# Narrow heads: stack reads spread over twice as many steps, the maxima's lead raised during the first batch, each stack piece read after its own half is stored

## The reference, cut to what matters

```python
HIDDEN, NUM_HEAD, GROUP = 256, 32, 8
HEAD_DIM = HIDDEN // NUM_HEAD            # 8
REP = NUM_HEAD // GROUP                  # 4
q = hidden_states @ Wq + bq              # (4, 512, 32 heads x 8)
k = hidden_states @ Wk + bk              # (4, 512,  8 heads x 8)
v = hidden_states @ Wv + bv
scores = einsum('bhqd,bhkd->bhqk', q, k) / sqrt(8)
attn = softmax(scores, axis=-1)          # no mask, all 512 x 512
out = einsum('bhqk,bhkd->bhqd', attn, v)
x = x + (out @ Wo + bo)
```

## Time and profile before

| | |
|---|---|
| median of 3 runs | 3807.46 us |
| the profiled execution | 3817.35 us, span 3815.6 us |
| TensorE busy (matmul) | 3340.4 us, 88% |
| VectorE busy | 2627.6 us, 69% |
| ScalarE busy | 1932.8 us, 51% |
| GpSimd busy | 993.4 us, 26% |
| the narrow-head phase: first stack read to last attend | 1257.7 to 1786 us |

### The profile page before, as it was taken

The page is one execution under the profiler, slowest core; times in us unless marked ns, Lnnn a source line. Parts: engine busy times, 40 slices in busy tenths (PEclk is TensorE's granted clock), DMA queues, the critical chain, the costliest instruction groups (busy, mean ns, idle before and its releaser), DMA issues. The chain is left out here.

```text
span 3815.6 us, 62869 instructions
## 1 busy us (share of the span) xinstructions
PE 3340.4 (88%) x21000; PEld 2195.9 (58%) x21002; DVE 2627.6 (69%) x8701; ACT 1932.8 (51%) x5261; POOL 993.4 (26%) x960
## 2 busy tenths in 40 slices
PE   6999999986995898998799999988699558999975
PEld 4666666653553433343567666765355347878864
DVE  6888888874443766774788888877344467777766
ACT  4667676653221355666466767665222115555531
POOL 3212121333443000011221212134344333222213
PEclk9999999997997678999899999998799769999986
DMA  4231300013654222110242310001565500000010
GB/s 125 78 136 55 112 1 1 33 48 122 150 90 100 65 47 56 43 29 17 74 132 82 110 58 1 1 34 59 158 121 88 127 14 15 1 15 4 1 33 23
DMA packets 201926, 234.63 MB, mean 61 GB/s; under 512 B 20358, under 2 KB 188232, under 8 KB 200776
## 3 DMA queue, kind: packets, MB, share of 16 engines
q1 hardware_dynamic: 170664, 190.48, 16.4%
q0 software_dynamic: 30944, 40.14, 6.2%
HBM read 98.13 MB, written 133.73 MB: 61 GB/s over the span
## 5 line engine op out<-in xcount | busy, mean ns | idle before, releaser
L1732 ACT ACTIVATE p_prob<-bank,p_small 128x256 f32<-128x256 f32 (+3 forms) x1280 | 647.4, 516 | 170.7 <-DVE p_small L1903 166.1
L1903 DVE CUSTOM_DVE_ANT_0 bank<-bank,p_mask 128x256 f32<-128x256 f32 (+3 forms) x1280 | 578.5, 489 | 93.5 <-PE bank L1475 82.6
L2248 POOL TENSOR_TENSOR p_tm<-p_rope_a,p_rope_b 128x512 f32<-128x512 f32 x192 | 246.5, 1284 | 1324.2 <-DVE p_rope_b L1883 1319.8
L1475 PE MATMUL bank<-p_k,p_q 64*128 64x256 f32 (+3 forms) x3840 | 528.0, 347 | 18.5 <-ACT p_prob L1732 17.3
L1737 ACT ACTIVATE p_prT<-bank 128x512 f32<-128x512 f32 x752 | 425.1, 601 | 197.7 <-PE bank L1484 196.3
L1484 PE MATMUL bank<-g_ident,p_prob 128*128 128x128 f32 x3008 | 440.2, 286 | 43.7 <-DVE p_prob L1912 18.8
L1912 DVE TENSOR_SCALAR p_prob<-p_prob,p_small 128x256 f32<-128x256 f32 (+3 forms) x1280 | 414.2, 387 | 11.3
L1493 PE MATMUL bank<-p_prT,p_v 128*64 128x512 f32 (+1 forms) x1504 | 420.4, 606 | 0.3 <-ACT p_prT L1737 0.3
L1484 PEld LDWEIGHTS bank<-g_ident,p_prob 128*128 128x128 f32 x3008 | 333.2, 143 | 138.6 <-issue 56.2
L1475 PEld LDWEIGHTS bank<-p_k,p_q 64*128 64x128 f32 (+1 forms) x3840 | 338.3, 188 | 119.8 <-issue 63.0
L1949 DVE TENSOR_REDUCE p_nmax<-bank 128x1 f32<-128x512 f32 x512 | 325.0, 684 | 108.7 <-PE bank L1534 103.4
(11 more groups left out here) (289 smaller groups left out, 6253.6 us busy)
## 6 DMA issues: line engine op xcount, KB each, us to landing
sorted<-p_blank SPq DMA_DIRECT2D x32, 2304.0 KB, 19.2
p_w<-in_L_ffn_w SPq DMA_DIRECT2D x96, 256.0 KB, 4.4
p_h_in<-sorted SPq DMA_DIRECT2D x158, 144.0 KB, 2.7
p_k_st<-k_saved SPq DMA_DIRECT2D x16, 288.0 KB
p_q_st<-q_saved SPq DMA_DIRECT2D x16, 288.0 KB
g_stage<-in_L_ffn_wq SPq DMA_DIRECT2D x8, 512.0 KB, 4.4
g_stage<-in_L_ffn_wo SPq DMA_DIRECT2D x16, 256.0 KB, 5.1
g_res<-first_sum SPq DMA_DIRECT2D x8, 512.0 KB, 7.2
```

Of the source, the lines that this page charges most:

```text
L1475: ins = pe.matmul(h.use.ap[:, 0:n], q[rows, at, :], k[rows, kp, o.g, keys], start=i == 0, stop=i == 2)
L1732: act.activation(s.prob.ap[:, 0:s.o.w], s.use.ap[:, 0:s.o.w], ACT.Exp, bias=sm[:, 0, j:j + 1], scale=-1.0, accum_out=sm[:, 1, j:j + 1]).th ...
L1903: dve.tensor_tensor_reduce(x, x, A.mask[:, A.mask.shape[1] - o.w:], -1.0, FAR, ALU.add, ALU.min, o.sm.ap[:, 0, h.j:h.j + 1]).then_inc(made)
```

## The change

Three edits, all in the narrow-head phase.

1. Between two steps of part 1 of the stack reads, the side stream yields four times, not two, in every batch but the first. So there are eight attend steps from one `r` to the next where there were four.
2. During batch 0, after every eighth attend step one extra step of maxima is recorded. The lead grows from 48 to 64 steps over the batch, and stays there.
3. A step of `small_stack` waits before its read of `q_saved` for the half that holds its own `r`, where it waited for all of it.

```diff
-                    s.b, s.k_saved, s.saved, s.free, s.groups, s.count = b, saved[0], saved, stack_read.get(b - 2), groups, stacked[b % 2][part]
+                    s.b, s.k_saved, s.saved, s.free, s.groups, s.count = b, saved[0], saved[1 + r // 2], stack_read.get(b - 2), groups, stacked[b % 2][part]
                     s.r, s.pace = r, pace[0]
                     if part and b:
-                        yield
-                        yield
+                        for _ in range(4):
+                            yield
...
                     next(peaks, None)
                     if n % 2:
                         next(side, None)
+                    if b == 0 and n % 8 == 7:
+                        next(peaks, None)
...
-            w.wait_ge(*s.saved)
+            w.wait_ge(s.saved)
```

## The result

The changed kernel takes 3842.6 us (median of 4 runs, 3833.65 to 3849.63); the kernel before, run beside it, 3807.09 us. The ratio is 1.0088, with a 95% interval of 1.0068 to 1.0108: **slower by 0.9%**, where a gain of 0.7% was forecast, and outside the range of 3771 to 3796 us. A ratio here isn't the quotient of the two medians, and it leaves out the runs that lie more than 1.5% above the fastest of their kernel, which are two of four in e10 (the profiled one is among them) and two of six in e11. The profiled execution took 3841.22 us.

A forecast was written before the change was run, and what follows sets the result against it. Bound by TensorE, slowed by three waits for the store's DMA and the low clock behind them. Terms -30.0 - 2.4 + 2.6 + 3.0 = -26.8 us from 3807.46 gave 3780.7 us, range 3771 to 3796.

The forecast's parts named there:

- What bounds the kernel: Narrow-head phase: TensorE's three waits for the store's DMA, 13.1 us, and the low clock behind them, 16.9 us.
- Wider spacing: Part 1 stack reads: steps 6.1 us apart for 3.8 us of data, so the queue empties between them; cost nothing.
- Longer lead: Stores of maxima: 14.7 us ahead in batch 0, 23 us later, against landings of 14.0 us; all three waits go.
- What they are worth: The three stretches with store waits: losses of 12.2, 10.1 and 7.7 us, together 30.0 us, all won back.
- The moved maxima: 16 maxima at 0.16 us each on TensorE: 2.6 us added in batch 0, given back in batch 3; sum nothing.
- sign by which the text would have called itself wrong: Attend still waiting for the store in batches 1 or 2, or TensorE waiting for VectorE's queue in batch 0.
- New short waits in batch 0: TensorE: 1.4 us for a `finish` behind a store in bank 7, two `qp` waits of 0.6 us; together 2.6 us.
- Falls of the clock: TensorE in batch 0: a short wait may begin a new clock fall costing 4.0 us; 3.0 us allowed.
- The half's wait: Start of batch 0: `q_saved` reads go out earlier, so the first maximum comes 2.4 us earlier (0 to 2.6).
- The first store is still late: Rival, batch 0: spreading reads doesn't shorten the store's landing, 12.2 us loss stays, 3792.9 us; chance 0.14.
- The waits go, the clock doesn't come back: Rival: other short idle times begin equal clock falls, only 12.9 us of idle won, 3794.6 us; chance 0.13.
- Slower: short waits begin long falls: Rival, batch 0 and preludes: seven short waits each begin a 7.1 us fall, 50 us lost, 3827 us; chance 0.05.

The follow-up runs named there:

- e10: The kernel before with the maxima taking `r` in the order 0, 1, 2, 3 in place of 2, 3, 0, 1: 4005.94 us, ratio 1.0356.
- e11: The kernel before with the maxima taking `r` in the order 3, 0, 1, 2 in place of 2, 3, 0, 1: 4044.53 us, ratio 1.0561.
- e13: The kernel before plus the extra maxima with `r` chosen to fit the attends, old read spacing and old wait: 3798.31 us, ratio 0.9982.
- e14: The change without its extra maxima, the same kernel as e4 on another chip: 3779.16 us, ratio 0.9931.
- e5: The change without its extra maxima, with a lead of 64 from the start in place of 48: 3817.42 us, ratio 0.9956.
- e16: The change without its extra maxima, with a lead of 56 from the start in place of 48: 3791.3 us, ratio 0.997.
- e4: The change without its extra maxima, so wider read spacing and the wait for the half stored: 3781.47 us, ratio 0.9931.
- e15: The whole change with `r` of the maxima chosen to fit the attends, the same kernel as e12, run beside e14: 3792.01 us, ratio 0.9967.
- e2: The kernel before with only the extra maxima in batch 0: 3852.73 us, ratio 1.0129.
- e9: The whole change with its 16 extra maxima in four groups of four, each behind the last attend of a quarter: 3825.11 us, ratio 0.9972.
- e12: The whole change, extra maxima at their places, only `r` of the maxima chosen to fit the attends beside them: 3825.39 us, ratio 0.9969.
- e1: The kernel before with only the wider spacing of the part 1 reads: 3790.98 us, ratio 0.9983.
- e8: The whole change with 16 pairs of 128-row filler matmuls of zeros added in batch 0: 3880.22 us, ratio 1.0112.

## Why the prediction was wrong

*What bounds the kernel* stands in part: the waits for the store and the low clock were both there, but the second didn't hang on the first alone (below). Where the change worked undisturbed, batches 1 to 3, the phase gave back 27 us, at clocks near 1.00.

*Wider spacing: right in its mechanism.* The steps of part 1 in batch 1 were 6 us apart, as worked out, and attend no longer waited for the store behind them. (In the slowed batch 0 they were 10 us apart.) SyncE's queue:

```profile
1533.46 0.29 SPq L2415 DMA_DIRECT2D p_k_st<-k_saved  x1
...
1539.37 0.29 SPq L2415 DMA_DIRECT2D p_k_st<-k_saved  x1
...
1545.74 0.29 SPq L2415 DMA_DIRECT2D p_k_st<-k_saved  x1
```

*Longer lead: right on the waits, wrong on the worth.* All three waits went, in the change and in e13. But e14 keeps waits of 6.5 us and by its ratio is faster than every kernel without them, though the intervals of e5 and e16 touch its own. "What they are worth" counted the wait and its low clock as one thing that goes away whole (-30.0 us). They aren't: in e4's profile the waits are as short as in e14's, 6.1 us, and the phase is as long as before (491.8 against 490.1 us to the end of the last exponential), because the clock was low again (0.76 in batch 0).

*The moved maxima: here the prediction failed.* The step was "One costs TensorE about 0.85 - 31.0 / 45 = 0.16 us ... Their sum is nothing as long as VectorE keeps up." I took 0.16 us for a matmul that lasts 0.79 us at half clock without asking how four fifths of it could vanish. Three things stand in its place:

- A maximum has no fixed price. Beside attends of other row groups it costs nothing (0.44 us with and without, above), so the 0.16 us were other work of the stretch. Where no group is free it costs its own time: by e15 an estimated 7 to 8 us for the sixteen extras, in place of 2.6. And 0.3 us come back at the end, not 2.6.
- An extra maximum shifts all those behind it. 48 of batch 0's 64 pairs collide, at 1.16 - 0.73 = 0.43 us each at half clock, some 21 us. In the trace of the change collisions and extras together come to about that, by an estimate from its groups: not every pair stood at half clock, and some extras ran beside a maximum that had to wait anyway.
- Batch 0 stays near the half clock, at 0.55 where it had 0.78. That is what is left of the 56 us, more than half of them.

e2 (slower by 1.3%), e10 and e11 (by 3.6 and 5.6%), e9 and e12 (the loss gone) show that the row groups are the cause of the loss, its part by the low clock included. How they hold the clock down isn't shown. Neither sign by which the text would have called itself wrong came: attend waited for no store in batches 1 and 2, and VectorE wasn't what held up batch 0.

*New short waits in batch 0: mis-sized, and small.* Taken as 1.4 us for the `finish` behind the store, measured 0.3; the two more waits for `qp` didn't come, the row fell from 6 to 5 waits. Missed was the growth of the wait of the store's transposes for VectorE, 7.2 to 11.5 us.

*Falls of the clock: wrong kind.* The text allowed 3.0 us for falls that waits begin. What came was a low clock of up to 85 us with TensorE busy nearly throughout. The profile before had such a stretch of 40 us behind the wait at 1364, and the text read it as the price of that wait alone.

*The half's wait: mis-sized.* The reads for `r` = 0 and 1 did go into the gap, and the last one for part 0 was issued 3.6 us after the first (1257.64 - 1254.00) where 6.1 stood before, 2.4 us sooner as worked out. But the first maximum came 8.0 us after the first read (1262.04 - 1254.00), where 8.7 stood: 0.7 us, not 2.4.

```profile
1254.00 1.03 SPq L2415 DMA_DIRECT2D p_k_st<-k_saved  x1
...
1257.64 0.65 SPq L2418 DMA_DIRECT2D p_q_st<-q_saved  x1
```

```profile
1262.04 0.80 PE L1536 MATMUL bank<-p_k_st,p_q_st 24*128 24x512 f32 x3 [6.86 <-DMA p_q_st<-q_saved]
```

The step took the last issue as the end. Issued closer together, the last read landed later after its issue: the maximum came 4.4 us behind it, against 2.6 before (1266.42 - 1263.78).

*The rivals.* "The first store is still late" fell: no wait in batch 0, the longest landing 6.9 us from a DMA's own issue, where it was 12.3 (the text's 14.0 counts from the first of a store's four DMAs). That batch was slowed, which helps a store; but e12 and e15, where it wasn't so much, have no such wait either, and longest landings of 7.6 and 7.5 us. Its reason, that a landing doesn't depend on how much is queued, is spoken against by e1: the spacing alone took the longest landing from 12.3 to 9.6 us, and e4 and e14 have 8.0 and 8.3. "The waits go, the clock doesn't come back" has the number of e12 and e15 (12.9 us is a ratio of 0.9966, they have 0.9969 and 0.9967), but not by its mechanism: in e15 the clock of batches 1 to 3 is 0.94, 0.99 and 1.00, and what is missing is lost in batch 0. "Slower: short waits begin long falls" had the sign and part of the size (3827 us against 3842.6), by a mechanism that wasn't there: that it came near is luck. I think a chance of 0.05 for slower was too low for an edit that shifts two hand-written sequences against each other, when nothing in the text had asked why they stood in that phase.

## What to carry to other kernels

Where two streams of matmuls with few rows run beside each other, their row groups are part of the schedule: before shifting one by a step, write down which rows stand beside which at every step of the period, and shift by a whole period or choose the rows to fit. When a matmul seems to cost a fifth of its own duration, don't carry that price elsewhere: a free row group makes it cost nothing, and without one it costs all of its time, even when every other pair fits. And once a transfer is spread so that it drains between steps, a longer lead on top of it may bring nothing: try each alone.

## What the runs showed of the hardware that was not expected

- Four matmuls of 24 or 26 rows and 512 columns at half clock take 0.73 us side by side in four row groups, and 1.16 us when two of them meet a group that is taken, with one collision as with two. At the full clock it is 0.44 us against 0.67 (e10) and 0.66 (e11).
- TensorE can be busy for 50.00 of 50 us (e2) and be granted 0.50 of its clock throughout; in e10 it was busy for 574.58 of 590 us at a mean of 0.58, and already in the kernel before for 35.00 of 35 us at 0.50. Idle time isn't the only thing that goes with a low clock here. Matmuls of 128 rows of zeros put between didn't raise it (e8, 0.54). What it is in the colliding order that goes with the low clock is not settled.
- The same kernel had medians of 3805.5 to 3807.5 us on some chips and 3835.7 to 3836.5 us on two others: 30 us, more than the change was meant to bring. Only runs beside each other could be compared. Between the profiles of e12 and e15, the same kernel, 12 us of the 28 lie ahead of the first exponential of this phase, 12 behind the last and 4 in it.
